# Pairs of heads stacked in two halves of TensorE's rows, and small constants gathered into two loads

## What is computed

```python
# layer 0, for each sample
self_feat = concat([x, q_of_the_condition]) @ W_self.T + b_self
for d in range(2):
    aff = (self_feat @ Wq[d].T) . (self_feat[:20] @ Wk[d].T)      # 16 heads
    w = softmax(where(adj_count > 0, aff, -9e15) + label_bias)
    out += (w @ self_feat[:20]) @ Wout[d]
x = x + relu(out)
# layer 1
nx = ada_rmsnorm(x, cond)
q, k, v = rope(nx @ wq + bq), rope(nx @ wk + bk), nx @ wv + bv
probs = softmax(q @ k.T / 4)                                      # 16 heads, 256 x 256 each
x = x + (probs @ v) @ wo + bo
nx = ada_rmsnorm(x, cond)
x = x + (gelu(nx @ w_gate) * (nx @ w_up)) @ w_down
```

## Time and profile before

| | |
|---|---|
| time, median of 3 runs | 511.89 us (508.91 to 515.19) |
| the profiled execution: time | 512.82 us |
| its span, first to last instruction | 511.0 us |
| busy share of PE, PEld, DVE, ACT, POOL | 88%, 77%, 63%, 48%, 53% |
| mean granted TensorE clock | 0.96 of full |
| chain that ended last, share by engine | PE 67%, DVE 12%, POOL 9%, issue 5%, DMA 4% |

### The profile page before, as it was taken

One profiled execution on the slowest core, in us unless ns is written; L12 is line 12 of the kernel. 1 busy time (PEld: TensorE's weight loads), 2 busy tenths in 40 slices (PEclk: granted clock), 3 DMA queues, 4 the chain that ended last, 5 costly groups with the idle time before them and its releaser, 6 DMA issues.

```text
span 511.0 us, 9893 instructions
## 1 busy us (share of the span) xinstructions
PE 450.1 (88%) x3728; PEld 391.5 (77%) x3728; DVE 321.6 (63%) x529; ACT 245.0 (48%) x472; POOL 270.3 (53%) x266
## 2 busy tenths in 40 slices
PE   0776766878899999989999998999899979999997
PEld 0674655757588789878979897889788957897896
DVE  1757666898689547936995597478834870840421
ACT  1144412434722884177436843675466328347431
POOL 4555588597745655654554583546831371132232
PEclk9985787999889999999999998999999999999999
DMA  6920264614320430053014401540032003210000
GB/s 177 339 112 3 96 109 158 182 32 155 106 52 3 127 104 22 22 175 101 22 58 106 135 2 44 106 149 0 4 119 89 3 18 129 63 45 2 21 22 22
DMA packets 35231, 41.30 MB, mean 81 GB/s; under 512 B 5872, under 2 KB 27888, under 8 KB 35056
## 3 DMA queue, kind: packets, MB, share of 16 engines
q1 hardware_dynamic: 35184, 40.67, 27.3%
HBM read 29.90 MB, written 10.49 MB: 79 GB/s over the span
## 4 chain that ended last, share of the span: by engine, by line
PE 67%; DVE 12%; POOL 9%; issue 5%; DMA 4%; ACT 2%; SPq 1%; DVEq 0%; POOLq 0%; ACTq 0%
PE ps L2109 33%; PE ps L2326 7%; PE ps L2341 6%; PE ps L2302 5%; PE ps L2152 4%; PE ps L2228 3%; PE ps L2212 3%; PE ps L2240 3%; PE ps L2179 2%; DVE nm L1650 2%; POOL aff L641 2%; POOL prob L662 2%; DMA vec<-cols 1%; PE ps L2353 1%; DVE aff L1569 1%
## 5 line engine op out<-in xcount | busy, mean ns | idle before, releaser
L1650 DVE TENSOR_REDUCE nm<-ps 128x2 f32<-128x512 f32 x128 | 83.9, 683 | 26.3 <-PE ps L2302 25.8
L2109 PE MATMUL ps<-splz,wh 128*128 128x256 f32 x512 | 96.3, 286 | 3.0 <-DVE ya L1642 1.8
L1047 ACT ACTIVATE ex<-ps 128x512 f32<-128x512 f32 x128 | 70.0, 598 | 35.4 <-PE ps L2326 33.7
L2109 PEld LDWEIGHTS ps<-splz,wh 128*128 128x128 f32 x512 | 79.3, 191 | 5.5 <-issue 4.7
L597 POOL TENSOR_TENSOR hs<-g,hs 128x512 fp32r<-128x512 f32 x32 | 42.0, 1316 | 72.3 <-ACT hs L1091 72.3
L2109 PE MATMUL ps<-splz,wl 128*128 128x256 f32 x256 | 72.3, 282 | 0.0
L2302 PE MATMUL ps<-kst,qst 96*128 96x256 f32 x256 | 51.6, 305 | 4.9 <-DVE nm L1650 4.0
L2109 PE MATMUL ps<-wh,hs 128*128 128x256 f32 x256 | 52.8, 286 | 0.7 <-POOL hs L597 0.7
L2326 PE MATMUL ps<-qst,kst 100*128 100x256 f32 x256 | 49.2, 303 | 2.7 <-DMA qst<-ex 2.5
L1694 DVE TENSOR_TENSOR g<-ps,g 128x512 f32<-128x512 f32 x32 | 22.0, 687 | 46.4 <-PE ps L2109 41.0
L2109 PEld LDWEIGHTS ps<-splz,wl 128*128 128x128 f32 x256 | 48.8, 191 | 0.0
(11 more groups left out here) (131 smaller groups left out, 997.1 us busy)
## 6 DMA issues: line engine op xcount, KB each, us to landing
qk_d<-ya SPq DMA_DIRECT2D x32, 256.0 KB, 3.9
qst<-qk_d SPq DMA_DIRECT2D x48, 128.0 KB, 2.5
kst<-qk_d SPq DMA_DIRECT2D x96, 64.0 KB, 2.4
ex<-wall SPq DMA_DIRECT2D x15, 256.0 KB, 6.8
aff<-adj SPq DMA_DIRECT2D x8, 440.0 KB, 3.9
res<-x SPq DMA_DIRECT2D x8, 256.0 KB, 2.7
xTs<-xT SPq DMA_DIRECT2D x8, 256.0 KB, 3.6
result<-res SPq DMA_DIRECT2D x8, 256.0 KB, 2.0
```

The lines of the kernel that those rows point to most:

```text
L1047: act.activation(ex[:, h % EXR], ps[:, h % 2].rearrange("p (c s) -> p c s", c=TC), ACT.Exp, scale=SCALE).then_inc(ex_ok.sem, 1)
L1650: dve.tensor_reduce(nm[:, :, h % 2, h // 2], ps[:, h % 2].rearrange("p (c s) -> p c s", c=TC), AX.X, ALU.max, negate=True).then_inc(mx_ok. ...
L2109: ins = pe.matmul(dst, lhs(a, k), rhs(c, k), start=first_ and n == 0 and m == 0, stop=last_ and n == len(ks) - 1 and m == 2, **kw)
```

## The change

Queries and keys are stacked alike: the three row groups of the even head of a pair in rows 0-47, of the odd head in rows 64-111, with ones (`kst`) and the two parts of the negated maximum (`qst`) in rows 48-49 and 112-113. `kst` has half its size and no zeros. `s` and `st` take a pair: four matmuls, by turns over rows 0-63 and 64-127 of the array (its tile is 64 rows by 128 columns), the even head in bank 0 and the odd in bank 1. They have the same number of matmuls as before, and the same columns. `s(p)` waits for both reductions of pair p-1, `st(p)` for both exponentials. The stacks are now 24 DMAs for each sample in place of 18, of the same bytes but for the queries, whose DMAs are split by head. `vec`, `cT` and `wb` are part of `consts`, `rope` and `bo` of `late`. The order of all five lists is a new one.

```diff
-        kst = sb("kst", [P, H, S], F32R)
+        kst = sb("kst", [P, PAIRS, S], F32R)
...
-            def q_stack(part, at, half):
+            def stack(into, which, part, at, half):
                 a, z = half * PAIRS // 2, (half + 1) * PAIRS // 2
...
+                    sent = (hi_out, lo_out)[part][which]
                     sp.wait_ge(sent.sem, sent.at(b))
                     for e in range(2):
...
+                        row = 64 * e + at
+                        sp.dma_start(into[row:row + DH, a:z, :].bitcast(FP32),
+                                     qk_d[part, which * D + 32 * a:which * D + 32 * z].rearrange("(q e r) s -> r q e s", e=2, r=DH)[:, :, e, :]
                                      ).then_inc(stack_in[half].sem, 16)
...
-                        at = 96 + 2 * e + part
+                        at = 64 * e + 3 * DH + part
...
             load_x(0)
-            weights("q0", 0)()
+            get_consts()
             load_xT(0)
-            get_consts()
-            get_wb()
-            load_x(1)
+            load_adj(0)
+            cond()
+            weights("qk", 0)()
             nz_store(0)
             weights("self", 0)()
-            cond()
-            load_adj(0)
+            weights("q0", 0)()
+            weights("g", 0)()
             nz_load(0)
-            nz_store(1)
-            get_vec()
...
-            def zeros(n):
-                def step():
-                    pool.memset(kst[0:96, n * H // 2:(n + 1) * H // 2, :].bitcast(FP32), 0.0).then_inc(zero_ok.sem, 1)
-                return step
+            def kones():
+                pool.memset(kst[:].bitcast(FP32), 1.0).then_inc(one_ok.sem, 1)
...
-            def s(h):
+            def pairs(p, rows, stationary, moving, signal):
+                for c in range(TC):
+                    for e in range(2):
+                        at = 64 * e
+                        ins = pe.matmul(ps[:, e, c * S:(c + 1) * S], stationary[at:at + rows, p, c * P:(c + 1) * P], moving[at:at + rows, p, :],
+                                        start=True, stop=True)
+                        if c == TC - 1:
+                            ins.then_inc(signal.sem, 1)
+
+            def s(p):
                 def step(b):
-                    bk = h % 2
-                    if h < 2:
-                        before(pe, ex_ok, b - 1, H - 1 + h)
+                    if p == 0:
+                        before(pe, ex_ok, b - 1)
...
-                        pe.wait_ge(mx_ok.sem, mx_ok.at(b, h - 1))
+                        pe.wait_ge(mx_ok.sem, mx_ok.at(b, 2 * p))
...
-                    for c in range(TC):
-                        ins = pe.matmul(ps[:, bk, c * S:(c + 1) * S], qst[0:96, h // 2, c * P:(c + 1) * P], kst[0:96, h, :], start=True, stop=True)
-                    ins.then_inc(s_ps.sem, 1)
+                    pairs(p, 3 * DH, qst, kst, s_ps)
...
-                        pe.wait_ge(ex_ok.sem, ex_ok.at(b, h - 1))
...
+                    else:
+                        pe.wait_ge(ex_ok.sem, ex_ok.at(b, 2 * p))
+                    pairs(p, 3 * DH + 2, kst, qst, st_ps)
```

More of the change, by code:

```diff
@@ L1716, in _ @@
             am(1)(0)
-            ones(0)()
             amax(1)(0)
@@ L2420, in _ @@
             selfm(1)(0)
+            small(1)(0)
             small(0)(0)
-            small(1)(0)
             kT(0)
@@ L2752, in _ @@
             gate(0, 1)(2)
+            x1T(5)
+            st(0)(3)
+            gate(1, 0)(2)
+            gate(1, 1)(2)
+            selfm(0)(6)
+            selfm(1)(6)
+            st(1)(3)
             up(0, 0)(2)
             up(0, 1)(2)
-            gate(1, 0)(2)
-            gate(1, 1)(2)
-            st(0)(3)
+            pv(0)(3)
+            st(2)(3)
+            small(1)(6)
+            small(0)(6)
             up(1, 0)(2)
-            st(1)(3)
             up(1, 1)(2)
+            st(3)(3)
@@ L2792, in _ @@
+            up(2, 1)(2)
             s(1)(4)
-            pv(3)(3)
+            oT(0)(3)
+            affm(0)(6)
             s(2)(4)
+            oT(1)(3)
+            gate(3, 0)(2)
+            affm(1)(6)
+            down(0, 0)(2)
+            down(0, 1)(2)
             s(3)(4)
-            affm(0)(6)
+            gate(3, 1)(2)
+            aT(3)
+            up(3, 0)(2)
             s(4)(4)
-            s(5)(4)
-            up(2, 1)(2)
-            affm(1)(6)
-            gate(3, 0)(2)
-            s(6)(4)
@@ L2880, in _ @@
+            up(2, 1)(3)
+            oT(0)(4)
+            s(2)(5)
+            gate(2, 1)(3)
             q0(0, 0)(7)
-            oT(0)(4)
             q0(0, 1)(7)
-            s(2)(5)
             q0(1, 0)(7)
             q0(1, 1)(7)
+            gate(3, 0)(3)
             oT(1)(4)
+            affm(0)(7)
             s(3)(5)
-            up(2, 0)(3)
+            aT(4)
+            down(0, 0)(3)
+            down(0, 1)(3)
+            down(1, 0)(3)
+            gate(3, 1)(3)
             s(4)(5)
-            affm(0)(7)
+            down(1, 1)(3)
@@ L2969, in _ @@
[L2969 to L2979 removed]
+            gate(2, 1)(4)
+            up(2, 1)(4)
+            st(7)(5)
+            y(7)
+            s(0)(6)
+            pv(3)(5)
+            gate(3, 0)(4)
+            up(3, 0)(4)
+            s(1)(6)
+            oT(0)(5)
+            x1T(7)
@@ L3072, in _ @@
             gate(0, 1)(6)
-            up(0, 0)(6)
-            up(0, 1)(6)
+            down(2, 0)(5)
             gate(1, 0)(6)
@@ L3187 @@
     mask4 = ((row[:, None] // MP == np.arange(4)) & (row[:, None] % MP < M)).astype(np.float32)
-    ones = ((row[:, None] - 96) // 2 == np.arange(H) % 2).astype(np.float32)
     bkrow = np.repeat(f["L0_cond_bk"].reshape(4, P), MP, axis=0)
```

1454 lines of the change are left out of this document (634 added, 820 removed).

## The result

The changed kernel takes 538.95 us (median of 5 runs, 534.26 to 541.68) against 511.89 before: the ratio is 1.0495, with a 95% interval of 1.0444 to 1.0545. It is slower, by 27 us; the forecast of 516 us and its range up to 532 were both too low. The profiled execution took 534.26 us, with a span of 532.5 (before: 512.82 and 511.0). Ratios and intervals leave out the executions that ran slow, among them one of 1440 us (lists_mend) and one of 1117 us (tiny_half) whose cause is not known; the medians are over all executions.

A forecast was written before the change was run, and what follows sets the result against it. PE was taken as the bound, about 0.75 us of time per microsecond of its work. 512.8 + 6.4 (form) - 2 (already idle) + 1 (both banks) - 2 (start) = 516 us, range 485 to 532.

The forecast's parts named there:

- Two halves at once: Score pair steps: row halves overlap, 0.24 us saved in each of 128 steps, -30.7 us of PE.
- The form: PE's order: 196 more changes of tile form at 0.20 us each, +39.2 us of PE.
- Their sum: -30.7 + 39.2 = +8.5 us of PE, times 0.75 +6.4 us; the -2 is less PE idle before score steps.
- The factor 0.75: From 100 to 475 us, a microsecond of PE work is worth about 0.75 us, PE's share of the chain.
- Both banks wait: Score steps wait for both reductions or exponentials of the pair before: +1 us; as rival slower, 526 us, chance 0.13.
- The start: Sample 0's start: `vec` in the second DMA and earlier weights bring `nzq` and `nzb` 1 to 3 us sooner, -2 us.
- The stacks' six more DMAs: Three more queries' DMAs before `s(0)`, 1.9 us a sample on SP, covered by its wait for the keys' store: 0.
- Free: Rival: halves of rows change form at no cost, PE loses 30.7 us of work; 490 us, chance 0.32.
- One after another: Rival: the row halves don't overlap but the form changes still cost; 540 us, chance 0.10.

The follow-up runs named there:

- lists_mend: Changed kernel with head by head score steps over the whole array, and the second conditioning weights' load moved ahead of sample 1's row-sum store: 520.1 us, ratio 1.0190.
- tiny_half: Kernel before plus one 8-column matmul over rows 0 to 63 ahead of each even head's score and transposed score step: 544.9 us, ratio 1.0670.
- same_half: Changed kernel with the second conditioning weights' load moved ahead, both products of a pair reading rows 0 to 63: 552.9 us, ratio 1.0795.
- tiny_full: Control: kernel before plus one 8-column matmul over rows 0 to 95 ahead of each even head's score and transposed score step: 518.7 us, ratio 1.0173.
- before_gather: Kernel before with only `vec`, `wb` and `cT` gathered into the constants' load, issued second: 511.3 us, ratio 1.0042.
- r_lists_mend: Same kernel as lists_mend, run again beside three others on one chip: 523.6 us, ratio 1.0175 to the kernel before.
- r_after_mend: Same kernel as after_mend, run again beside three others on one chip: 531.8 us, ratio 1.0367 to the kernel before.
- after_mend: Changed kernel with one SyncE line moved: second conditioning weights' load ahead of the store of sample 1's row sums: 531.6 us, ratio 1.0349.

## Why the prediction was wrong

The measured steps on one chip: lists and loads +9.0, both banks +2.9, the form +6.9, the held start +5.2; together 24 us (the first measurement had 27), where the forecast had 4 (516 against 511.9). The prediction failed at the two terms outside PE's sum, the new lists and the start; its sum for the form came out.

- **Two halves at once, -30.7 us of PE: right.** 0.50 us for four matmuls where same_half has 0.73, and 23 us of span, just the forecast.
- **The form, +39.2 us of PE: right in rule and price.** Rows 0-63 change the form as columns do; the price is 0.195 in and out between products, where 0.20 was taken from `pv` and `y`. The number of changes is right too: PE's order in the two traces has 96 and 292. The Trainium skill, "TensorEngine Tiling (Array Packing)", section Key Properties, states that changing the tiling mode drains TensorE (the modes, 64 rows by 128 columns among them, stand under Available Configurations, just ahead of it); tiny_half against tiny_full, 26 us for 225 changes, shows the cost for rows, which no row before the change could.
- **Their sum: right within what was measured.** +6.4 - 2 = +4.4 us was forecast, 6.9 with 3 us of uncertainty measured. The factor 0.75 stands: same_half gave 0.74, the small matmuls about 0.8. That the sum agrees to 2.5 us is in part luck, with an uncertainty of 3 us.
- **Both banks wait, +1: the size holds in the new lists, the working does not.** 2.9 us there, with 3 us of uncertainty, but 29 to 30 in the old lists, above the bound of +26. The step that failed is the round "two reductions of 0.68, the pair 0.24 and a bare load": what PE waits for is VectorE's list, with other work ahead of the second reduction, 1.75 us at the place shown. That the new order keeps this from PE, as "most pair steps have 1.5 to 3 us of other work between them" had it, fits the 2.9 us; which feature of the order does it is not shown.
- **The new lists: not priced at all, +9.0, the largest term.** The step that failed is the term that isn't there: the forecast took the new order and the gathered loads to be neutral but for sample 0's start. The gathered constants are neutral within 4 us (before_gather), so it is mostly the order, if the untested load `late` costs nothing. Which of the moved steps does it stays open. The queue that still stands behind sample 2's row sums is a candidate that the traces show; how much of the 9 us is its work no run tells.
- **The start, -2: wrong in sign, +5.2.** The step that failed is "Next late is `nzb`, ... and the products `selfm`": I followed sample 0 only. That gain came (14.73 in place of 17.04) and is worth nothing by itself, as before_gather shows. Next late was the second conditioning layer, whose weights stand behind a store that waits for another engine's list. I read how far each load had moved, not what the line ahead of it waits for. With the lists' 9.0 the two terms outside the sum make 14 of the 24 us.
- **The stacks' six more DMAs, 0: nearly.** They are inside the form's 6.9 us. PE waits for a keys' stack only twice, in the changed kernel as in r_lists_mend_both, 1.4 us longer (1.9 in r_after_mend). The lists of waits of the one and the other (us, times, longest):

```profile
PE ps L2268 <- DMA kst<-qk_d: 4.0, 2, 2.9
```

```profile
PE ps L2296 <- DMA kst<-qk_d: 2.6, 2, 2.1
```

- **The rivals.** "Free" is excluded by tiny_half, "one after another" by the pair's 0.50 us. "One after another", at 540, was nearest to the measured 539, by luck alone: its mechanism is the one that the traces exclude. "Both banks wait", at 526, names a mechanism that in the old lists is dearer than feared; here it makes 2.9 of the 24 us. The range ended at 532 to leave out the case of 540, and every case in it shared the same start and the same neutral lists. The last sentence had named that ("if the new lists order the ramp otherwise than the old"), but with "a few us either way" and no chance.

## What to carry to other kernels

A step that writes two banks at once turns two buffers into one: price its wait by the reader's whole list between the two reads, and look for an order that has other work between the steps. The Trainium skill, "Perfetto Trace Analysis", section Matmuls, advises to rotate independent groups of matmuls through the banks, so that reading one overlaps the next group; here the loss of that rotation cost 30 us in one order of work and 3 us in another. A smaller form has to save more than it pays for going in and out: one pair step between products saved 0.24 us and paid 0.39. And of a queue that issues in order, read for each load what the line ahead of it waits for, and go on to the next such line when one is mended.

## What the hardware showed

- Matmuls over rows 0-63 and 64-127 of different banks run at once: four in 0.50 us where the same four in one half take 0.73. Their weight loads run at once too: the 512 loads of the scores keep PEld busy for 39.3 us in the changed kernel, 74.2 before.
- A change of form between 128 and 64 rows costs PE 0.195 us each way between products of 256 columns, and 0.27 to 0.29 for in and out together around a matmul of 8 columns.
- The same 32 matmuls of 8 columns took 7.00 us at a granted clock of 0.50 (the level of 1.2 GHz), behind 6.93 us of waiting (the changed kernel); 6.97 at 0.50 behind 1.07 of waiting (r_after_mend); 5.06 at 0.71, again behind 1.07 (after_mend). The first and the last, as windows of the two traces:

```profile
35.28:42.28 7.00, 7.00 (x33) 7.00 (x34) 0.56 (x2) 0.00 (x0) 1.05 (x1) 0.50 0.25 95
29.96:35.02 5.06, 5.06 (x32) 4.97 (x32) 2.03 (x4) 2.48 (x3) 4.13 (x4) 0.71 0.79 198
```
